# One GpSimd product of four states in place of two products of two, for the last two pairs of each channel group

## The reference, cut to what matters

```
# xs = (delta, Bm, Cm, u), s is [batch, 512 channels, 16 states], 1024 time steps
def step(s, inp):
    d_t, B_t, C_t, u_t = inp
    dA  = exp(d_t[..., None] * A)                     # the decay
    dBu = d_t[..., None] * B_t[:, None, :] * u_t[..., None]   # the drive
    s = dA * s + dBu
    y_t = einsum('bdn,bn->bd', s, C_t)                # weigh and sum
    return (s, y_t)
```

## Time and profile before

| | us |
|---|---|
| three runs | 2281.25, 2282.62, 2284.83 |
| median | 2282.62 |
| the profiled execution | 2281.53 |
| its span, first to last instruction | 2279.7 |
| TensorE busy in the span | 2103.7 (92%) |
| VectorE | 2021.2 (89%) |
| GpSimd | 1969.3 (86%) |
| ScalarE | 1685.4 (74%) |

### The profile page before, as it was taken

One profiled execution on the slowest core, in us unless ns is written; L12 is line 12 of the kernel. 1 busy time (PEld: TensorE's weight loads), 2 busy tenths in 40 slices (PEclk: granted clock), 3 DMA queues, 4 the chain that ended last, 5 costly groups with the idle time before them and its releaser, 6 DMA issues. The chain is left out here.

```text
span 2279.7 us, 45508 instructions
## 1 busy us (share of the span) xinstructions
PE 2103.7 (92%) x13263; PEld 1713.8 (75%) x13263; DVE 2021.2 (89%) x2844; ACT 1685.4 (74%) x3447; POOL 1969.3 (86%) x1252
## 2 busy tenths in 40 slices
PE   8889899999999998989898989999977999999996
PEld 5667677777777777767677777777767999999885
DVE  5999999999999999999999999999998556657776
ACT  6787879788888888887879788888774544445664
POOL 3988999999999999999999999999997576667775
PEclk9999999999999999999999999999998999999998
DMA  6041414233232415051414142332316677668886
GB/s 192 2 158 46 151 53 153 67 130 102 95 123 74 146 59 175 22 177 38 158 53 144 64 142 72 125 111 85 120 67 212 114 129 156 128 101 162 183 182 153
DMA packets 226007, 263.59 MB, mean 116 GB/s; under 512 B 101123, under 2 KB 182563, under 8 KB 225636
## 3 DMA queue, kind: packets, MB, share of 16 engines
q1 hardware_dynamic: 175172, 208.07, 29.9%
q0 software_dynamic: 29904, 34.77, 8.5%
q10 hardware_dynamic: 20688, 17.85, 2.6%
HBM read 196.75 MB, written 71.71 MB: 118 GB/s over the span
## 5 line engine op out<-in xcount | busy, mean ns | idle before, releaser
L897 POOL TENSOR_TENSOR dbu<-drive_u,w_all 128x1024 f32<-128x1024 f32 x384 | 904.0, 2365 | 45.6 <-DVE ps_a L753 27.6
L1210 ACT ACTIVATE ps_a<-delta,a_neg 128x512 f32<-128x512 f32 x768 | 518.3, 685 | 113.0 <-DVE area L753 98.2
L914 POOL TENSOR_TENSOR wp<-area 128x1024 f32<-128x1024 f32 x192 | 453.1, 2360 | 8.6 <-DVE area L753 8.1
L765 DVE TENSOR_TENSOR wd<-ps_a,area 128x1024 f32<-128x1024 f32 x320 | 383.7, 1199 | 0.0
L1476 PEld LDWEIGHTS ps_y<-ident,wd 128*128 128x128 f32 x2560 | 304.7, 145 | 99.1 <-issue 71.0
L1476 PE MATMUL ps_y<-ident,wd 128*128 128x128 f32 x2560 | 341.6, 279 | 14.5 <-DVE wd L765 14.3
L2059 POOL DMA_INDIRECT acc_scratch<-ow,e_meta x135 | 220.9, 1636 | 132.0 <-DVE ow L1970 120.9
L1503 PEld LDWEIGHTS ps_a<-dg,duT 128*128 128x128 f32 x2048 | 250.8, 198 | 58.5 <-issue 57.3
L1503 PE MATMUL ps_a<-dg,duT 128*128 128x128 f32 x2048 | 260.8, 282 | 30.1 <-ACT carry L1217 27.8
L2301 PEld LDWEIGHTS e_ps_h<-xT,w_tile 128*128 128x128 f32 x2160 | 260.6, 192 | 16.2 <-DVE xT L1948 10.2
L2301 PE MATMUL e_ps_h<-xT,w_tile 128*128 128x128 f32 x2160 | 266.3, 277 | 2.1 <-DVE xT L1948 1.9
(11 more groups left out here) (247 smaller groups left out, 3825.9 us busy)
## 6 DMA issues: line engine op xcount, KB each, us to landing
area<-b_scratch SPq DMA_DIRECT2D x128, 512.0 KB, 4.9
w_all<-b_scratch SPq DMA_DIRECT2D x96, 512.0 KB, 4.0
dg<-xs_scratch SPq DMA_DIRECT2D x540, 32.0 KB
area<-in_L_attn_x_dram SPq DMA_DIRECT2D x32, 512.0 KB, 5.2
ee<-acc_scratch SPq DMA_DIRECT2D x32, 512.0 KB, 4.1
x_scratch<-area SPq DMA_DIRECT2D x16, 512.0 KB, 2.9
acc_scratch<-area SPq DMA_DIRECT2D x16, 512.0 KB
area<-x_scratch ACTq DMA_DIRECT2D x32, 256.0 KB
```

The lines of the kernel that those rows point to most:

```text
L765: dve.tensor_tensor(wd[:, s % NWD], states(k, 2), cc[:, n:n + 2, :], ALU.mult).then_inc(wd_done, 1)
L897: pool.tensor_tensor(dbu[:, k % NBU], du[:, g % 2, :].unsqueeze(1).broadcast_to([P, 2, CH]), bb[:, row:row + 2, :], ALU.mult).then_inc(dbu ...
L914: pool.tensor_tensor(wp[:, s % 2], ss[:, s % 2], cc[:, rows, :], ALU.mult).then_inc(wp_done, 1)
L1210: act.activation(dst, dl[:, g, :], ACT.Exp, scale=a_neg[:, g, n:n + 1]).then_inc(exp_done, 1)
```

## The change

In every channel group but the first, the products of pairs 6 and 7 become one product over four states, 128x2048. It waits for what both of the old ones waited for, and raises `dbu_done` by two at its end. Its place in GpSimd's order is that of pair 6.

```diff
+        TWO = (6,)
...
+            def times_b_two(t, m):
+
+                c, g = t // G, t % G
+                k = t * HB + m
+                row, slot = 2 * brow(m), k % NBU
+                if g == 0:
+                    pool.wait_ge(b_in[m], 16 * (c + 1))
+                    pool.wait_ge(b_in[m + 1], 16 * (c + 1))
+                if m == 0:
+                    pool.wait_ge(du_done, t + 1)
+                pool.wait_ge(scan_done, 2 * (k + 1 - NBU) + 2)
+                pool.tensor_tensor(dbu[:, slot:slot + 2].rearrange("p a h n -> p (a h) n"),
+                                   du[:, g % 2, :].unsqueeze(1).broadcast_to([P, 4, CH]),
+                                   bb[:, row:row + 4, :], ALU.mult).then_inc(dbu_done, 2)
...
-                if t <= LAST and m not in BMS:
+                if t <= LAST and m not in BMS and (t == 0 or m not in (*TWO, *(a + 1 for a in TWO))):
                     times_b(t, m)
+                if 0 < t <= LAST and m in TWO:
+                    times_b_two(t, m)
```

## The result

The changed kernel takes 2306.05 us (median of 4 runs, 2302.74 to 2307.82), the kernel before 2283.72 (2281.25 to 2286.74). The ratio is 1.0093, with a 95% interval of 1.0079 to 1.0108: slower by some 22 us. The forecast was 2283.1, with a range to 2290. The profiled execution took 2307.4 us with a span of 2305.8, against 2279.7.

A forecast was written before the change was run, and what follows sets the result against it. VectorE's scans were taken to pace the stage, with GpSimd running ahead. GpSimd's saving 0, state 12 0, turned pairs 0.5 and loads 0 sum to 0.5 us: 2282.62 + 0.5 = 2283.1 us, range 2279 to 2290.

The forecast's parts named there:

- What bounds the kernel: Scan stage: VectorE's stream of scans sets the pace and GpSimd runs ahead, so sparing GpSimd work can hardly win time.
- GpSimd's saving: Merged products in 63 channel groups: GpSimd is spared 11.5 us, counted as 0 because VectorE does not wait for it.
- The margin ahead of state 12: Double product's end to its scan: at least 0.4 us left, 0.85 to 1.1 mostly with g = 1 and 3; cost 0.
- The rival that was built on it: Double product ends after state 12's scan should start: 2289 us at 5.0 us, 2300 at 5.3; chance 0.05.
- The loads: Loads waiting for the double product: pair 6's up to 5.5 us later, pair 7's up to 2.2; counted as 0.
- the signal: End of pair 6: known only when all four states are done, with state 12's scan waiting for it; counted as 0.
- The weighed states: GpSimd's weighed pairs come later and TensorE turns them in fixed order, so VectorE is delayed: 0.5 us taken.
- late turns reach the scans: Slower rival: the late weighed pair costs 0.9 us in all 15 groups with g = 0, 13.5 us, 2296; chance 0.07.
- The faster rival: VectorE's waits for ScalarE and TensorE come from GpSimd in the end: up to 11.5 us won, 2271; chance 0.05.
- the one of a held port: A running GpSimd instruction holds VectorE, longer with each double product: 69 us, 2352; chance 0.01.
- The signs to look for: Changed profile: product 4.54 us, GpSimd some 11 us less busy, VectorE's waits within 3 us, TensorE's weighed-pair wait 20 to 30.
- more waits of L753 for L1503: Sign against the forecast: VectorE's scans wait more for TensorE's drive, showing TensorE's lateness.

The follow-up runs named there:

- the late signal: Kernel before, with pairs 6 and 7 told done together at the end of pair 7, in all channel groups but the first: 2285.23 us, ratio 1.0001.
- the sooner W2 on the old kernel: Kernel before, with one scatter (g = 0) and one convolution addition (g = 1) moved behind W2 in GpSimd's order: 2285.85 us, ratio 1.0002.

## Why the prediction was wrong

- **What bounds the kernel, and 4.54 us for the product:** right. (The 4497 ns that the prediction cites from the Trainium skill stand there for an addition; the product took 4541 ns, 1% more.) VectorE paces the stage, never waits for the double product, and GpSimd's saving was not a gain.
- **The margin ahead of state 12:** right to some 0.1 us (forecast 0.85 to 1.1 us with g = 1 and 3, read 0.73 to 1.06), but for t = 9 and 57, where 0.4 was forecast and 0.74 and 0.75 were read. The rival that was built on it did not come, and "VectorE does not wait for GpSimd" was taken to settle too much.
- **The loads, the signal:** right at 0; the late signal alone measured 1.0001.
- **"The weighed states", with "counted directly, VectorE loses 0.15 us in the whole stage by late turns. I take 0.5 us":** this is the step that failed. It measured some 22 us. The mechanism was named and its size was missed, three times over.
  1. *How late W2 is.* The prediction makes it 1.2 us late in t = 28, "some waits of GpSimd having taken up the rest". It is 1.8 us late there: it ends 4.50 us after the start of state 0, before 2.73. Between the double product and this W2 GpSimd is idle only ahead of two scatters, 0.16 and 0.17 us before, 0.15 and 0.17 after. These gaps are no waits and take up nothing: both the double product and W2 are 1.8 us late. In the median W2 became 2.1 us late in g = 0 and 1.3 in g = 1.
  2. *How far the lateness runs.* It was followed from W2 to the drive of states 4 and 5 and to the gate, and dropped there. In g = 1 nothing on TensorE absorbs it up to the drive of states 10 and 11, and the margin at its end was 0.57 us or none. On the way it also reaches ScalarE, and through it the decay of state 9. The two make 9.2 of the 25.7 us of the profiled execution, with g = 1 alone.
  3. *The clock.* That a shift of TensorE's order can change where the low clock falls, and so bring stalls of 1.5 us each, was in no rival: 6 more such stalls make 9 of the 25.7 us of this execution. How much it is in an average run is not shown.
- **The rival "late turns reach the scans"** had the right path and 13.5 us, with 0.07. Its place, state 4 with g = 0, was wrong: that scan lost next to nothing, and it was states 10 and 9 with g = 1.
- **The faster rival and the one of a held port** got no support: the wide product and two narrow ones in its place are not told apart (1.0093 and 1.0105).
- **The signs to look for** told it. GpSimd's busy time, the product's time and the missing row of GpSimd came as written. TensorE's wait for weighed pairs grew from 11 to 49 us where 20 to 30 was written, VectorE's waits grew by 20.5 us where at most 3 was written, and "more waits of L753 for L1503", named as what would prove the forecast wrong, came: 8.7 to 23.1 us.

No version here beats the kernel before; three are level with it: the late signal, the sooner W2 on the old kernel, and the double product in g = 1 and 2 alone.

## What to carry to other kernels

When two instructions are merged, the merged one inherits the later of the two starts. If the engine is the one that feeds others, follow what stands behind it on that engine, not only its own result. A path through a third engine has to be walked to the end of that engine's gapless stretch, and into every engine that it feeds on the way: lateness is used up only by a wait, and a small regular gap ahead of an instruction is not a wait until it shrinks when the engine is late. The margin that counts is the one at the last place reached, here 0.57 us after eleven us of solid work on TensorE.

## What the runs showed of the hardware that was not expected

- GpSimd's product of 128x512, 128x1024 and 128x2048 takes 1273, 2363 and 4541 ns: linear to 2 ns, with 183 ns that do not depend on the width. A wide one running had no effect on the scans: one without a carry takes 1185 to 1225 ns beside it, before 1184 to 1225.
- Ahead of most scatters of GpSimd (92 of 116, before 87 of 120) lie 0.14 to 0.17 us that are for the most part put down to "issue" and that don't shrink when GpSimd is late. Where one scatter stands behind another, it is 0.30 us.
- The granted clock of TensorE fell to 0.50 without any idle time before it (eight of the nine falls, none of over 0.05 us for 33 us), behind matmuls of 8 columns. The stalls from it went from 3 to 9 with a change that touches no instruction of TensorE, while the falls in the scan stage went from 22 to 26 only, and to 2 with four matmuls of 128 columns a chunk added.
